# Key-by-key products ahead of layer 0's queries, query products behind V, and other filler products in a one-core vision tower

## The reference

```python
def delta_attn(x, Wq, Wk, Wv, Wb, Wo, onorm_w):
    q = l2norm(silu((x @ Wq).reshape(b, t, H, DK)))
    k = l2norm(silu((x @ Wk).reshape(b, t, H, DK)))
    v = silu((x @ Wv).reshape(b, t, H, DV))
    beta = sigmoid(x @ Wb) * 2.0
    def step(S, inps):
        qi, ki, vi, bi = inps
        pred = einsum('bhkv,bhk->bhv', S, ki)
        S = S + bi[..., None, None] * ki[..., :, None] * (vi - pred)[..., None, :]
        return S, einsum('bhkv,bhk->bhv', S, qi)
    S0 = jnp.zeros((b, H, DK, DV), x.dtype)
    _, o = jax.lax.scan(step, S0, (qt, kt, vt, bt))
    o = rmsnorm(o, onorm_w)
    return o.reshape(b, t, H * DV) @ Wo
for l in range(2):
    x = x + delta_attn(rmsnorm(x, norm1_w[l]), ...)
    g, y = split(rmsnorm(x, norm2_w[l]) @ Wg[l])
    x = x + silu(g) * y @ Wd[l]
```

## Time and profile before

| what | value |
|---|---|
| median of 3 runs | 298.28 us (295.71 to 298.95) |
| the profiled execution | 297.97 us |
| its span | 296.2 us, so 1.8 us lie around it |
| PE busy | 269.8 us, 91% |
| DVE busy | 207.1 us, 70% |
| ACT busy | 92.9 us, 31% |
| PE's share of the chain that ended last | 69% |
| DVE's share of it | 24% |
| mean granted clock of TensorE | 0.942 |

### The profile page before, as it was taken

One profiled execution on the slowest core, in us unless ns is written; L12 is line 12 of the kernel. 1 busy time (PEld: TensorE's weight loads), 2 busy tenths in 40 slices (PEclk: granted clock), 3 DMA queues, 4 the chain that ended last, 5 costly groups with the idle time before them and its releaser, 6 DMA issues.

```text
span 296.2 us, 9893 instructions
## 1 busy us (share of the span) xinstructions
PE 269.8 (91%) x4465; PEld 208.1 (70%) x4465; DVE 207.1 (70%) x414; ACT 92.9 (31%) x230; POOL 37.9 (13%) x35
## 2 busy tenths in 40 slices
PE   8999999999999899988898999987899899499865
PEld 8666678778997787957785776767877576365442
DVE  3649869978688744467677669675667664597992
ACT  1222301320000115555325432656324433231210
POOL 1981100202992000000000000000000000000000
PEclk9999999999999959889978999979987999869999
DMA  7999900000000000000001302500000000000001
GB/s 294 414 424 423 431 8 0 0 0 2 0 0 2 1 0 3 2 2 2 2 4 17 129 0 69 233 4 2 1 4 2 2 0 0 1 0 0 2 0 44
DMA packets 2730, 18.71 MB, mean 63 GB/s; under 512 B 464, under 2 KB 784, under 8 KB 1936
## 3 DMA queue, kind: packets, MB, share of 16 engines
q1 hardware_dynamic: 2704, 18.34, 15.6%
HBM read 18.01 MB, written 0.33 MB: 62 GB/s over the span
## 4 chain that ended last, share of the span: by engine, by line
PE 69%; DVE 24%; issue 3%; DMA 2%; ACT 2%; SPq 0%; DVEq 0%; ACTq 0%
PE ps L1248 12%; PE ps L1565 8%; PE ps L1292 5%; PE ps L1306 4%; PE ps L1546 3%; PE ps L1673 3%; PE ps L1664 2%; PE ps L1775 2%; DVE big L1100 2%; DMA big<-in_patches 2%; DVE wt L1097 2%; PE ps L1724 2%; PE ps L1695 2%; PE ps L1238 2%; PE ps L1817 2%
## 5 line engine op out<-in xcount | busy, mean ns | idle before, releaser
L1248 PE MATMUL ps<-big,cwb 128*128 128x384 f32 x112 | 37.9, 489 | 0.0
L1248 PEld LDWEIGHTS ps<-big,cwb 128*128 128x128 f32 x112 | 20.9, 190 | 13.0 <-DVE cwb L704 0.3
L1565 PE MATMUL ps<-xT,wl 128*128 128x320 f32 x88 | 24.5, 434 | 2.3 <-DVE xT L1142 2.3
L288 POOL TENSOR_TENSOR xs<-xs,big 128x640 f32<-128x640 f32 x14 | 23.3, 1666 | 1.4
L1565 PEld LDWEIGHTS ps<-xT,wl 128*128 128x128 f32 x88 | 16.6, 190 | 9.4 <-ACT wguT L368 2.7
L1664 PE MATMUL ps<-wt,big 32*32 32x32 f32 x1280 | 14.2, 194 | 5.3 <-DVE big L1100 2.8
L344 ACT COPY pecT<-ps 128x384 f32<-128x384 f32 x12 | 5.8, 480 | 40.7 <-PE ps L1248 40.7
L1664 PEld LDWEIGHTS ps<-wt,big 32*32 32x32 f32 x1280 | 12.4, 104 | 7.5 <-DVE big L1100 4.5
L1306 PE MATMUL ps<-wt,pecT 128*128 128x256 f32 x72 | 16.5, 380 | 0.6 <-DVE big L809 0.6
L1292 PE MATMUL ps<-wt,pecT 128*128 128x256 f32 x72 | 16.9, 381 | 0.0
L1306 PEld LDWEIGHTS ps<-wt,pecT 128*128 128x128 f32 x72 | 13.5, 190 | 3.0 <-DVE big L809 1.0
(11 more groups left out here) (301 smaller groups left out, 540.8 us busy)
## 6 DMA issues: line engine op xcount, KB each, us to landing
big<-in_patches SPq DMA_DIRECT2D x6, 960.0 KB, 11.7
wl<-in_layers SPq DMA_DIRECT2D x2, 2176.0 KB, 19.7
wf<-in_ffn SPq DMA_DIRECT2D x1, 2112.0 KB, 17.8
wl<-in_layers SPq DMA_DIRECT2D x2, 1040.0 KB, 15.9
wt<-in_tok SPq DMA_DIRECT2D x1, 1536.0 KB, 24.7
wt<-in_tok SPq DMA_DIRECT2D x1, 768.0 KB, 8.5
cwb<-in_conv SPq DMA_DIRECT2D x1, 640.0 KB, 3.9
cst<-in_constants SPq DMA_DIRECT2D x1, 320.0 KB, 25.0
```

What stands on the lines that cost most here:

```text
L288: nc.gpsimd.tensor_tensor(xs[:, hf], old, new, ALU.add).then_inc(S["xsum"], 1)
L1248: last = mm(ps[:, i % 4, 0:GRP], cwc[:, k, c * P:(c + 1) * P], xg[:, g, k, :], start=(k == 0), stop=(k == KC - 1))
L1565: last = mm(ps[:, bank, 0:NT], w(c, j), x[:, c, :], start=(c == 0), stop=(c == CH - 1))
```

## The change

- `per_window` is split in two passes of 40 products with 64 moving columns each. The pass for keys (`per_window(0, ...)`) stands behind `key_squares()` and waits for nothing that `key_squares` did not wait for; the pass for queries (`per_window(1, ...)`) stands behind V and waits for the second `silu` and for both key scalings of DVE (`ap` of 2).
- In layer 0 the query projection moves behind the key pass. In layer 1 it stays ahead of betas.
- Bank numbers: queries' projection in 4 and 5 (3 and 4 before), beta in bank 7 (5 before), the sum of squares in bank 6 (0 before), all window products in banks 0 to 3. ACT's copy of window pair 4 and its semaphore `p5` are gone, and DVE's scalings of pairs 3 and 4 become one instruction.
- ACT takes the tanh of beta ahead of the silu of queries.
- Fillers: the 36 opening products of 32 x 64 become 4 of 128 x 512; counts 5, 4 and 3 of 64 columns become 2, 2 and 2 of 128 columns; two of 128 x 320 in layer 1 become 18 of 32 x 48.

```diff
@@ scalar, layer(l)
                 silu_kq(0)
                 act_.wait_ge(S["silu"], EACH["silu"] * l + 1)
                 nc.scalar.activation(kqsq[:, 0], skq[:, 0], ACT.Square).then_inc(S["silu"], 1)
+                act_.wait_ge(S["b_mm"], EACH["b_mm"] * l + 1)
+                nc.scalar.activation(tb, ps[:, 7, C:C + NG], ACT.Tanh, scale=0.5).then_inc(S["silu"], 1)
                 silu_kq(1)
-                act_.wait_ge(S["b_mm"], EACH["b_mm"] * l + 1)
-                nc.scalar.activation(tb, ps[:, 5, 0:NG], ACT.Tanh, scale=0.5).then_inc(S["silu"], 1)
-                act_.wait_ge(S["ap_mm"], EACH["ap_mm"] * l + 1)
-                nc.scalar.copy(apm[:, 16:NG, :], ps[:, 4:8, 0:P]).then_inc(S["p5"], 1)
@@ vector, layer(l)
-                dve.wait_ge(S["ap_mm"], EACH["ap_mm"] * l + 2)
+                dve.wait_ge(S["ap_mm"], EACH["ap_mm"] * l + 1)
                 keys_scaled(0, 3)
                 pairs(0)
-                keys_scaled(3, 1)
-                dve.wait_ge(S["p5"], EACH["p5"] * l + 1)
-                keys_scaled(4, 1)
+                keys_scaled(3, 2)
                 pairs(1)
@@ tensor
-            def keep_clock_briefly(bank, n):
+            def keep_clock_briefly(bank, n, width=P):
 
                 for _ in range(n):
-                    mm(ps[0:32, bank, 0:64], ones[:, 0:32], ones[:, 0:64], start=True, stop=True)
+                    mm(ps[0:32, bank, 0:width], ones[:, 0:32], ones[:, 0:width], start=True, stop=True)
 
             pe.wait_ge(S["ones"], 1)
-            keep_clock_briefly(7, 36)
+            for _ in range(4):
+                mm(ps[:, 7, :].rearrange("p (k n) -> p k n", k=4), ones[:, :], ones[:, :].unsqueeze(1).broadcast_to([P, 4, P]),
+                   start=True, stop=True)
...
-            keep_clock_briefly(4, 5)
+            keep_clock_briefly(4, 2)
...
             keep_clock(4, 1)
-            keep_clock_briefly(4, 4)
+            keep_clock_briefly(4, 2)
...
-                    keep_clock(0, 2)
+                    keep_clock_briefly(0, 18, 48)
...
-                    keep_clock_briefly(4, 3)
+                    keep_clock_briefly(4, 2)
@@ tensor, layer(l)
-                for j in range(CH):
-                    last = project_cols(3 + j, L_Q, j, slice(0, NT), src)
-                last.then_inc(S["kq_mm"], 1)
+                    queries()
...
-                pe.wait_ge(S["silu"], EACH["silu"] * l + 4)
-                per_window(4).then_inc(S["ap_mm"], 1)
+                per_window(0, (0, 64, 128, 192, 256))
+                if l == 0:
+                    queries()
                 pe.wait_ge(S["ss"], EACH["ss"] * l + 1)
-                for pj in range(4):
-                    last = per_window(pj)
-                last.then_inc(S["ap_mm"], 1)
-
-                pe.wait_ge(S["p5"], EACH["p5"] * l + 1)
+                pe.wait_ge(S["silu"], EACH["silu"] * l + 3)
...
                 last.then_inc(S["v_mm"], 1)
+                pe.wait_ge(S["silu"], EACH["silu"] * l + 4)
+                pe.wait_ge(S["ap"], EACH["ap"] * l + 2)
+                per_window(1, (320, 384, 448, 0, 64))
```

More of the change, by code:

```diff
@@ L527, in layer @@
                 y_out(3, 1)
-                act_.wait_ge(S["silu"], EACH["silu"] * l + 3)
+                act_.wait_ge(S["silu"], EACH["silu"] * l + 4)
                 nc.scalar.activation(kqsq[:, 1], skq[:, 1], ACT.Square, scale=(DH * EPS_RMS) ** 0.5
@@ L1594, in layer, with queries @@
                 last.then_inc(S["kq_mm"], 1)
+                def queries():
+                    for j in range(CH):
+                        last = project_cols(4 + j, L_Q, j, slice(0, NT), src)
+                    last.then_inc(S["kq_mm"], 1)
                 if l:
                     pe.wait_ge(S["h1"], 4)
-                for j in range(CH):
-                    last = project_cols(3 + j, L_Q, j, slice(0, NT), src)
-                last.then_inc(S["kq_mm"], 1)
+                    queries()
                 def betas():
@@ L1604, in betas @@
                         for c in range(CH):
-                            last = mm(ps[:, 5, H * p:H * p + H], hT[:, c, P * p:P * p + P], wb[:, c, :],
+                            last = mm(ps[:, 7, C + H * p:C + H * p + H], hT[:, c, P * p:P * p + P], wb[:, c, :],
                                       start=(c == 0), stop=(c == CH - 1))
@@ L1617, in key_squares @@
                         p = pj // 2
-                        mm(ps[:, 0, HP * pj:HP * pj + HP], kqsq[:, 0, pj % 2, P * p:P * p + P], heads, start=True, stop=True)
+                        mm(ps[:, 6, HP * pj:HP * pj + HP], kqsq[:, 0, pj % 2, P * p:P * p + P], heads, start=True, stop=True)
                     for a in range(2):
-                        last = mm(ps[64 * a:64 * a + 64, 0, 4 * HP:5 * HP], kqsq[:, 0, a, NW:NT], heads, start=True, stop=True)
+                        last = mm(ps[64 * a:64 * a + 64, 6, 4 * HP:5 * HP], kqsq[:, 0, a, NW:NT], heads, start=True, stop=True)
                     last.then_inc(S["ss_mm"], 1)
@@ L1626, in layer, with per_window @@
                 key_squares()
[L1628 to L1640 removed]
+                def per_window(k, col):
+                    for pj in range(PJ):
+                        for a in range(2):
+                            sq_, j = (2 * (pj // 2) + a, pj % 2) if pj < 4 else (4, a)
+                            for h in range(HP):
+                                r = slice(DH * h, DH * h + DH)
+                                at = slice(IMGS * sq_, IMGS * sq_ + IMGS)
+                                last = mm(ps[64 * a:64 * a + 64, h, col[pj]:col[pj] + 64],
+                                          skq[r, 0, j, at], skq[r, k, j, at], start=True, stop=True)
+                    last.then_inc(S["ap_mm"], 1)
+                per_window(0, (0, 64, 128, 192, 256))
+                if l == 0:
+                    queries()
                 pe.wait_ge(S["ss"], EACH["ss"] * l + 1)
[L1642 to L1646 removed]
+                pe.wait_ge(S["silu"], EACH["silu"] * l + 3)
                 for c in range(CH):
```

39 lines of the change are left out of this document (14 added, 25 removed).

## The result

| | before | changed |
|---|---|---|
| median | 297.93 us (4 runs, 295.71 to 298.95) | 307.36 us (4 runs, 305.09 to 309.37) |
| ratio | 1 | 1.0332, 95% interval 1.0275 to 1.0389 |
| profiled execution, its span | 297.97, 296.2 us | 309.37, 307.6 us |
| PE busy | 269.8 us | 277.9 us |
| mean granted clock | 0.942 | 0.911 |

A forecast was written before the change was run, and what follows sets the result against it. The prediction took PE to bound the kernel, with page borders of 256 instructions stopping it in the loops. 297.97 - 0.35 (middle fillers) + 0.15 (layer 1 filler) + 2.0 (layer 1) + 0.6 (layer 0) = 300.4, median 300.7 us; range 296.2 to 303.2.

The forecast's parts named there:

- What bounds the kernel now: PE, busy 269.8 of 296.2 us; stops of 0.61 and 0.51 us in the first z are borders of 256-instruction pages.
- Where the borders fall: After 22 MATMULs of layer 0's query pass, 70 of first y, 38 of first z; layer 1: 29, 77, 45.
- Entering to ready: From PE entering a page until the next one is ready: 1.1 + 1.0 + 1.25 us, 3.35 us in all.
- The sign that it gave for being wrong: First and second y run through without a stop, or 16 KB transfers come closer than 3.3 us.
- Layer 0: Page waits up to the first z: 0 or +1.4 us, taken as +0.6, bounds -0.25 to +1.5.
- rival B: Pages bind and the clock is lost longer: layer 0 +2.8, layer 1 +3.0, sum 303.7 us; chance 0.15.
- Layer 1: +2.0, bounds to +3.0: Pages ready at 200.45 and 203.8 delay DVE's masked copy from 202.28 to 204.25: +2.0 us, bounds +1.2 to +3.0.
- Its sign: Sign of being right in layer 1: DVE's first masked copy of the loop comes 6.4 to 7.2 us after `ap`.
- The clock: Ahead of layer 0's loop, full or half clock in queries: page entered at 126.7 or 128.2, costing 0 or +1.4 us.
- Fillers: Opening costs 0 us (bounds 0 to +0.8); middle groups ahead of the loop save 0.35 us (bounds -0.5 to 0).
- The layer 1 filler: Ahead of layer 1's keys, 36 MATMULs of 48 columns end at 184.55: +0.15 us, bounds 0 to +0.8.
- A: Rival: pages do not bind and the new order pays; 295.8 to 298 us, middle 296.9; chance 0.25.

The follow-up runs named there:

- b_tiny40: The kernel before with 40 tiny unused products (160 instructions) behind V in both layers; 305.55 us, ratio 1.0329.
- b_pages: The kernel before with 320 tiny unused products (1280 instructions, 5 pages) behind PE's last product; 311.11 us, one execution, beside 297.64.
- a_again: The changed kernel unaltered, measured once more; 304.85 us, ratio 1.0173 to the kernel before.
- b_opening: The kernel before with only the opening changed: 36 fillers of 32 x 64 become 4 of 128 x 512; 303.80 us, ratio 1.0271.
- b_idle: The kernel before with two unused DVE additions of 704 columns ahead of its second key scaling in both layers; 299.90 us, ratio 1.0115.
- b_open40: The kernel before with 40 in place of 36 opening fillers, 16 instructions more; 301.92 us, ratio 1.0103.
- b_open32: The kernel before with 32 in place of 36 opening fillers, 16 instructions fewer; 297.12 us against 297.64, ratio 0.9962.
- b_open24: The kernel before with 24 in place of 36 opening fillers, 48 instructions fewer; 303.01 us, ratio 1.0154.

## Why the prediction was right in kind and wrong in size

*What bounds the kernel now.* Right. The two stops were page borders, and the page size was right: every stop of 0.4 us or more with the cause "issue" in the first rounds of every run here lies within two MATMULs of a count by 256.

*Where the borders fall.* Right at the four stops, to within one MATMUL. That a border falls in the query pass and asks for the next page too late is what b_tiny40 shows with products that do nothing.

*Entering to ready, 3.35 us.* Too small. Where one stop follows another by a page, in the first rounds and in b_pages, the restarts lie 3.34 to 4.00 us apart (17 cases in ten runs, 3.73 in the middle): 3.94 and 3.87 in the first profile of the changed kernel, 3.34 and 3.87 in the second (a_again), 3.73 to 4.00 in b_pages. The prediction's value came from one transfer of 1.0 us; they take 0.9 to 1.4 in the loops. The sign that it gave for being wrong, transfers closer than 3.3 us, is met by a hair twice in the second profile (3.26), where the stops stand all the same.

*Layer 0: "the border in the query pass is entered while V runs, 126.7 ... 128.2".* **This is the step that failed.** With queries ending at 125.6 and V at the full clock (2.5 us), the pass itself starts near 128.1 by the prediction's own times, so 126.7 puts the entering of the page some 1.8 us ahead of the instruction at the border, the 22nd MATMUL of the pass. There is no such lead. The transfer that belongs to this border starts at 132.63, 1.1 us after PE had reached it (131.24 + 0.29), and in the second profile 0.9 us after (127.54, against 126.34 + 0.29). From a restart to the next transfer it is mostly 1.0 to 1.2 us, at most 1.7, so the page was entered about when PE came to it, and not 1.8 us before. Counted from the class columns, the page that the first y needs was to be ready after 12.0 us at the full clock; it was ready after 16.4 in the first profile and 14.7 in the second. Of these 4.5 and 2.7 us, 1.8 and 1.6 are the lead that was not there, and 2.7 and 1.1 are PE's own, since the pass started later: queries took 4.0 and 3.2 us and not 2.2, part of it at half the clock (rival B's term). By the prediction's times the first page is ready at 130.05 when the first y needs it near 130.0, so they imply next to no first stop and a second of 1.9 us; measured are 1.86 and 2.00. Up to the second round it is +5.7 us where +0.6 was taken, and in the second profile, where the clock was 0.50 ahead of the loop only from 118.9 to 122.3, 115.25 to 135.25, 20.0 against 16.7 us, +3.3. So the layer costs 3.3 to 5.7, and the bounds -0.25 to +1.5 were wrong even without much of the clock.

A border closer to V can be entered early: in b_opening, layer 1, it lies four MATMULs into the loop, and its transfer starts at 199.28, while V runs. So the prediction's idea holds for a few instructions and not for the 44 in question.

*Layer 1: +2.0, bounds to +3.0.* Mis-sized; measured +3.9, in the second profile +3.8. From the start of the query pass to the first page ready it is 3.94 us and to the next 3.87, where 3.35 was taken each time; V's first product ran at half the clock (2.08 us for four MATMULs, 1.65 before), so the pass started 0.6 us later than forecast. The stops are 2.02 and 2.52 us in place of the 1.05 and 1.9 that the times of the prediction imply. Its sign, DVE's first masked copy 6.4 to 7.2 us after `ap`, came at 9.1 and 9.0 us.

*The clock.* The prediction weighed it ahead of the loop alone, at queries and V. It had no term for what a stop does to it. The granted clock falls behind the stops, at 134.9 and 209.9 in the first profile of the changed kernel and at 132.5 and 204.2 in the second, and stays at 0.50 for 7 to 10 us, where in the earlier trace rows it is 1.00 through the first round. How much is it? Over 38 executions of the kernel before, time against the time spent at 0.50 (twice one less the mean granted clock, times the execution) is a line of slope 0.32; over the 8 of the changed kernel the slope is 0.325. The kernel before spends 34.1 us there on the mean, the changed one 45.7. 11.6 x 0.325 = 3.8 of the 8.1 us between the two means (298.0 and 306.1) go with the clock, 4.3 with everything else. The stops less what they replaced come to 5.2 us in the first profile and 5.0 in the second. So the two parts don't add up cleanly, and the split rests on a fit, not on an experiment that holds the clock. How much of the clock's part the stops themselves bring about stays open: b_opening and b_tiny40 have it with the stops, b_idle does not have it with an idle of 3.25 us.

*Fillers.* The middle ones save little: four MATMULs of 128 columns take 0.55 us on the chain, not 0.43, and the class columns start 0.1 us later than before (forecast: 0.35 earlier), as do the first patches. The layer 1 filler takes 1.65 us for 36 of 48 columns until the keys start, and the keys start 2.4 us after the transposes' start where it was 2.05: +0.3, for +0.15. The opening ends at 6.74 and costs nothing by itself, as said, but moves every later border by 128 instructions, which was counted.

*Rivals.* A fell with the stops. B named half of what happened in layer 0 in one of two profiles. B's own sum is 0.2 us off: 297.97 - 0.2 + 5.8 is 303.6 against the execution and 303.9 against the median, not 303.7.

The Trainium skill, Runtime: NRT & Kernel Launch, section Instruction fetch mechanics, gives 16 KiB blocks of 256 instructions, which every run here bears out. That a crossing is mostly hidden holds here where 256 instructions take longer than the 3.34 to 4.00 us of a page (the kernel before has 20 transfers and two stops of over 0.4 us with this cause); in b_pages each costs 1.85 to 2.41 us.

No version beat both kernels beyond its interval. 32 opening fillers in place of 36 come nearest, at 0.9962 (0.9924 to 1.0001).

## What to carry to other kernels

Count PE's instructions, not only its time. Where products are so small that 256 instructions (64 products of fp32 here, each with its loads) run in less than the 3.3 to 4.0 us that a page took here, the stream itself is the bound, and 40 small products in front of a dense loop cost far more than their 0.8 to 1.1 us. Don't count on the stream being read far ahead: here a page was asked for when PE came to the border in front of it, or a few instructions before. An edit far away, a filler more or less, moves every page border behind it: so compare the position of stops whose cause is "issue" before believing that a reordering was good or bad, and try the same edit at two or three shifts.

## What the runs showed of the hardware that was not expected

- Borders of pages are 256 instructions apart to within two MATMULs over a whole kernel, and 16 instructions more at the start bring a stop of 2.14 us in a loop 200 us later (b_open40).
- A page is entered past a waiting instruction when it lies 7 instructions behind it and not when it lies 23 or 39 behind (b_open32, b_open24, one case each).
- The granted clock fell to 0.50 in the first round behind both idles of 3.25 us in b_idle, and behind stops of 1.7 to 2.0 us in both profiles of the changed kernel. The time at 0.50 over the program grew with page stops (34.1 to 45.3 us in b_opening) and not with those idles (34.2).
- The stop at one border of one stream was 0.61 us in one execution and 1.72 in another, with the wait ahead of it 1.01 and 0: the wait and the stop trade places (the kernel before, b_pages).
